# A conditioned residual kernel: the table load, the condition row and the first four loads of x change their DMA queues, and the table is read in runs of 512 B

## The reference

```python
W = weights[condition]                       # (64, 128, 128) chosen out of (16, 128, 128)
x = x + einsum('bct,bcd->bdt', x, W)         # x: (64, 128, 2048), float32
```

## Time and profile before

| | us |
|---|---|
| median of 3 runs | 320.15 (319.94 to 320.36) |
| the profiled execution's own time | 320.04 |
| its span, first to last instruction | 318.3 |

### The profile page before, as it was taken

One profiled execution on the slowest core, in us unless ns is written; L12 is line 12 of the kernel. 1 busy time (PEld: TensorE's weight loads), 2 busy tenths in 40 slices (PEclk: granted clock), 3 DMA queues, 4 the chain that ended last, 5 costly groups with the idle time before them and its releaser, 6 DMA issues.

```text
span 318.3 us, 1351 instructions
## 1 busy us (share of the span) xinstructions
PE 246.5 (77%) x512; PEld 104.6 (33%) x512; DVE 146.8 (46%) x65; POOL 18.9 (6%) x69
## 2 busy tenths in 40 slices
PE   0099999991996979779398895939979596796960
PEld 0044444440442424334143342414424242342420
DVE  0026766762252553735237362641626556055460
POOL 0000000000010000001000010000000001000000
PEclk9999999998796998999779799996979999598996
DMA  8999999999999999999999999999999999999997
GB/s 329 416 441 457 371 424 457 397 461 399 457 424 432 449 408 461 412 445 432 424 453 404 457 424 432 445 412 461 399 457 424 432 449 408 461 395 461 420 411 298
DMA packets 5187, 135.29 MB, mean 425 GB/s; under 512 B 578, under 2 KB 578, under 8 KB 578
## 3 DMA queue, kind: packets, MB, share of 16 engines
q1 hardware_dynamic: 2448, 68.16, 50.0%
q10 hardware_dynamic: 2738, 67.11, 48.9%
HBM read 68.16 MB, written 67.11 MB: 425 GB/s over the span
## 4 chain that ended last, share of the span: by engine, by line
DMA 61%; PE 33%; DVE 3%; issue 0%; SPq 0%
PE product L92 33%; DMA out<-x_ring 32%; DMA x_ring<-x 30%; DVE x_ring L108 3%; SPq L58 0%
## 5 line engine op out<-in xcount | busy, mean ns | idle before, releaser
L92 PE MATMUL product<-x_ring,chosen_weights 128*128 128x512 f32 x512 | 246.5, 644 | 61.4 <-DMA x_ring<-x 61.4
L108 DVE TENSOR_TENSOR x_ring<-product,x_ring 128x2048 f32<-128x2048 f32 x64 | 146.7, 2291 | 161.4 <-PE product L92 161.4
L92 PEld LDWEIGHTS product<-x_ring,chosen_weights 128*128 128x128 f32 x512 | 104.6, 207 | 202.4 <-issue 122.7
L80 POOL COPY chosen_weights<-weight_table 128x128 f32 x64 | 18.7, 293 | 284.6 <-DVE x_ring L108 277.7
L102 DVE TENSOR_SCALAR state_row<-condition_row 1x64 int32<-1x64 int32 x1 | 0.2, 182 | 2.0 <-DMA condition_row<-condition 2.0
L137 POOL MEMSET const-float32-0.0<- 128x1 f32 x1 | 0.1, 98 | 0.1
L137 POOL MEMSET const-bfloat16-1.0<- 128x1 bf16 x1 | 0.1, 101 | 0.0
L137 POOL MEMSET const-uint8-127<- 128x1 uint8 x1 | 0.1, 101 | 0.0
L137 POOL MEMSET const-float32-1.0<- 128x1 f32 x1 | 0.1, 98 | 0.0
L137 POOL BASE_LOAD x1 | 0.0, 12 | 0.1
## 6 DMA issues: line engine op xcount, KB each, us to landing
x_ring<-x SPq DMA_DIRECT2D x16, 4096.0 KB, 26.7
out<-x_ring ACTq DMA_DIRECT2D x15, 4096.0 KB, 31.3
out<-x_ring ACTq DMA_DIRECT2D x4, 1024.0 KB, 9.1
weight_table<-weights SPq DMA_DIRECT2D x1, 1024.0 KB, 4.9
condition_row<-condition ACTq DMA_DIRECT2D x1, 0.2 KB
```

Of the source, the lines that this page charges most:

```text
L80: pool.tensor_copy(chosen_weights[b][:, :], weight_table[:, bass.ds(state[b] * features, features)]).then_inc(weights_chosen[b], 1)
L92: last = pe.matmul(product[:, b % psum_slots, m * BANK_COLUMNS:(m + 1) * BANK_COLUMNS], chosen_weights[b][:, :], x_ring[:, bass.ds(b * tim ...
L108: dve.tensor_tensor(tile, product[:, b % psum_slots, :], tile, AluOpType.add).then_inc(sum_done[b], 1)
```

## The change

Three things, all in which queue issues what and in which order, and in the layout of the table:

- The condition row is loaded by SP, as its first and only DMA ahead of the loads. It was ACT's first.
- The host leaves the table as it is given, states outermost. The load of it is now issued by ACT, as ACT's first DMA. For a partition the 128 floats of one state are one run of 512 B in HBM, and the sixteen runs of a partition stand 64 KB apart; so the read has 2048 runs of 512 B where it had 128 of 8 KB. The destination in SBUF is the same.
- ACT issues the loads of the first four groups behind the table, and only then goes on to the stores. SP's loop begins with the fifth group, each load behind its wait as before.

Nothing is changed on Pool, PE and VectorE, nor in the stores.

```diff
-    _, states, features = weights.shape
+    states, _, features = weights.shape
...
         def _(sp):
-            sp.dma_start(weight_table[:, :], weights.rearrange("c s d -> c (s d)")
-                          ).then_inc(table_loaded, 16)
-            for g in range(groups):
+            sp.dma_start(condition_row[0:1, :], condition.rearrange("(o b) -> o b", o=1)
+                          ).then_inc(condition_loaded, 16)
+            for g in range(ROOMS, groups):
                 room = g % ROOMS
-                if g >= ROOMS:
-                    sp.wait_ge(room_stored[room], 16 * (g // ROOMS))
+                sp.wait_ge(room_stored[room], 16 * (g // ROOMS))
                 sp.dma_start(x_ring[:, room * group_columns:(room + 1) * group_columns], x[g]
-                             ).then_inc(x_loaded[g % ROOMS], 16)
+                             ).then_inc(x_loaded[room], 16)
...
         def _(act):
-            act.dma_start(condition_row[0:1, :], condition.rearrange("(o b) -> o b", o=1)
-                          ).then_inc(condition_loaded, 16)
+
+            act.dma_start(weight_table[:, :].rearrange("c (s d) -> c s d", s=states),
+                          weights.rearrange("s c d -> c s d")).then_inc(table_loaded, 16)
+            for g in range(ROOMS):
+                act.dma_start(x_ring[:, g * group_columns:(g + 1) * group_columns], x[g]
+                              ).then_inc(x_loaded[g], 16)
...
-        "weights": np.ascontiguousarray(np.asarray(L0_cond_weights).transpose(1, 0, 2)),
+        "weights": np.ascontiguousarray(L0_cond_weights),
```

## The result

| | before | after |
|---|---|---|
| median of 10 runs, us | 320.21 | 321.36 (320.63 to 322.19) |
| the profiled execution, us | 320.04 | 322.04 |
| its span, us | 318.3 | 320.3 |
| table issued, landed, us | 0.79, 5.7 | 0.84, 7.0 |
| first matmul, us | 15.44 | 17.53 |

The ratio after to before is 1.0037 (95% interval 1.0022 to 1.0053, 0.7 to 1.7 us): slower by 1.15 us in the medians.

What follows compares the result with a forecast made beforehand. The prediction took the DMA engines, full almost throughout, to bound the kernel. To 320.15 us it added 1.0 for the table's short reads and 0 for all else: 321.15, rounded to 321.2 us, range 320.1 to 323.0.

Steps and rivals of the forecast that it cites:

- The sign it set itself: Whole kernel: if the span moves by more or less than the first matmul, the order of stores and loads has a price.
- the dear rival: Table's load at the start: short reads limited by their way to HBM, landing after 7.5 us, +1.6 to +2.8 us; chance 0.20.
- The bound: Whole kernel: the DMA engines set the time by packets times their length, whatever their order; 433 GB/s from 120 to 270 us.
- The table's read, +1.0: Table's load at the start: 128 reads of 512 B an engine take 3.5 us in place of 2.5, without cover.
- next to nothing: Rival on the table's load: a packet's fixed part is 0 to 4 ns or hidden, +0 to 0.5 us; chance 0.22.
- bound by their way to HBM: Rival on the table's load: short reads move at 197 GB/s or with descriptors made no faster, 321.8 to 323 us; chance 0.20.
- Who issues the table, 0: Kernel start: SP's and ACT's first issues both begin at 0.79 us, so moving the table to ACT costs 0.
- The condition row, 0: Kernel start: SP sends it at 0.79 us as ACT did, with 5 us of cover before it is needed; 0.
- The first four loads, 0: ACT's queue ahead of the stores: shifts what is queued, not how much; load 4 lands 3 us earlier, off the path; 0.
- The end, 0: Last stores: older stores queued ahead cover the last piece even if PE comes 1 us later; 0 us.
- faster rival: Last stores, 300 to 316 us: deeper queued stores remove the 0.5 us idle, -0.5 us, 319.7 us; chance 0.05.
- The engines run dry behind store 0: After the first store: the second is issued too late to keep the DMA engines busy, 1 to 3 us on top; chance 0.03.

Runs made afterwards that it cites:

- the short runs alone: The kernel before with only the table laid states outermost and read in 2048 runs of 512 B, still issued by SP: 321.21 us, ratio 1.0023.
- the order alone: The changed kernel with the table kept in its old layout, so only queues and order differ from before: 320.36 us, ratio 0.9997.
- the reads in the middle of the kernel: Three spare table reads behind the loads of groups 6, 8 and 10: 332.78 us in 512 B runs (changed kernel), 329.52 in 8 KB runs (old table layout).
- the load-ahead kernel: The changed kernel with ACT issuing the load of group 0 ahead of the table: 320.53 us, beside 321.29 for the changed kernel.

## Why the prediction was right, point by point

- **The sign it set itself.** The span was to move by as much as the first matmul. In after's profile it did (2.0 and 2.09 us), in the second profile of the same kernel it moved by 1.4 and the first matmul by 1.70, with the short runs alone by 0.7 and 1.26. The forecast 1.0 for the first matmul was too small, and a part of the shift is made up until the end. The reason named for such a difference, a price of the order, is not the one: the order alone cost 0.07 us in the medians. The table landed 6.2 us after its issue (5.9 was expected, 7.5 would have meant the dear rival).
- **The bound.** Right. The rate of 120 to 270 us is 433 GB/s before and after, and the order alone is worth 0.9997.
- **The table's read, +1.0.** The price of a run was right: 0.009 us split off beforehand, 0.0095 and 0.0091 measured, 1.14 us a table where it moves among others of its kind. Beside stores, by the reads in the middle of the kernel, such a table cost only 0.5 us. As a term of this sum it was too large. I charged the short reads in full against an old read of 2.5 us, but the old read, first of all, takes longer too: its packets ran from 1.79 to 5.31 us in before, 3.5 us. The short reads lose 0.4 to 0.7 us more than it, and part of that again until 100 us. Of the rivals' conditions, "next to nothing" fell, and "bound by their way to HBM" fell: 291 GB/s was held for 10 us, where it had 197.
- **Who issues the table, 0.** Wrong, and it is the term that fills the gap. It compared SP with ACT, where there is indeed no difference (0.83 us on either), and left the number of runs aside: I had allowed for a longer issue only as a delay of the loads behind, not of the table's own first packet. It makes the first data packet 0.67 us late, and costs 0.76 us in all by the load-ahead kernel.
- **So the sum** of 1.0 + 0 stands for measured parts of some 0.4 and 0.8, with 1.15 in total. The number was right partly by luck, because the two misses are opposite.
- **The condition row, 0.** Right: VectorE had it at 2.01 us.
- **The first four loads, 0.** Right in the time. In detail: load 3 landed at 46.7 us in after (45.5 was expected), store 0 20.6 us after its issue (20.5). Load 4 was to land at 76 us and came at 80.34, no earlier than before but for the shift. I had given load 4 half the engines from its issue to its landing, and forgotten that it starts late (its first packet began at 60.3 us, 3.8 after its issue), is confirmed late, and that store 1 has all of them until then. It was off the path that sets the end.
- **The end, 0, and its faster rival.** Nothing was won there: the last piece took 7.4 us in after, 7.6 before. "The engines run dry behind store 0" did not come about: store 1 was issued at 49.7 us and store 0 landed at 56.5.

## What to carry to other kernels

In a kernel that fills the DMA engines, price a layout by runs for each engine: here 0.009 us a run beyond its bytes where nothing but such reads moves, whether runs share a packet or not, so 512 B cost a third of the rate and 1 KB a sixth; beside stores it was 0.004. The DMA of 2048 runs was also long in being issued, so let such a one not be the first thing on an idle set of engines: one long load ahead of it took back 0.76 us of 1.1. And keep it on the queue of the loads that it must not wait for: with runs of 8 KB a queue of its own cost nothing, but with 512 B, against packets of 32 KB, the same table took 45 us to land and cost 26 us.

## What the runs showed of the hardware that was not expected

- 2048 runs of 512 B were moved as 512 packets of 2 KB, while 1024 runs of 1 KB were moved as packets of 1 KB, at 291 and 353 GB/s.
- The issue of the 2048-run DMA took 0.83 us on SP and ACT alike, that of 1024 runs 0.43 us and of 128 runs 0.37 to 0.38 us; issues behind queued tables took longer, up to 3.1 us in the kernel with four tables of 512 B and 2.8 us with four of 1 KB.
- Short reads beside stores moved at 432 GB/s in all and cost 0.5 us a table; with no store beside, 325 GB/s and 1.1 us.
- Two queues were served 218 packets to 218 at up to sixteen times the packet size, but the queue whose first issue ended first had the engines for itself, for 2.8 and 4.2 us.
- Once or twice between 30 and 80 us some seventeen to thirty-two load packets take up to 2.4 us for 1.2, on kernels whose table has long runs; on those with short runs less is lost, or nothing. The cause is open.
